# Gated edges of a graph network: one product of 96 rows, four gather buffers, and another wait for GpSimd

## What is computed

```
concat = jnp.concatenate([h[src], h[dst], edge_attr], axis=-1)
gates = jax.nn.sigmoid(concat @ W_e + b_e)
messages = jax.nn.softplus(concat @ W_n + b_n)
gated = gates * messages
h_new = jax.ops.segment_sum(gated, dst, num_segments=n)
edge_count = jnp.clip(edge_count, 1.0, None)[:, None]
return h + h_new / edge_count
```

## Time and profile before

| | us |
|---|---|
| median of 3 runs | 3195.6 (3194.36 to 3196.31) |
| profiled execution, its own time | 3192.49 |
| its span | 3190.5 |
| busy: TensorE, VectorE, ScalarE, GpSimd | 2649.9, 1684.4, 1362.8, 905.0 |
| line 1136, 804 gathers | 766.6 busy |
| line 1349, 1620 records of matmul | 587.0 busy |
| line 1182, 135 adds | 183.8 busy, 402.2 idle before them |

### The profile page before, as it was taken

How to read it: one execution, slowest core, us unless ns; L and a number is a source line. 1 busy time by engine, 2 the same in 40 slices (tenths; PEclk the granted TensorE clock), 3 DMA queues, 4 the chain that set the end, 5 groups by cost and what they waited for, 6 DMA issues and landing times. The chain is left out here.

```text
span 3190.5 us, 66017 instructions
## 1 busy us (share of the span) xinstructions
PE 2649.9 (83%) x21196; PEld 2400.0 (75%) x21197; DVE 1684.4 (53%) x3606; ACT 1362.8 (43%) x2809; POOL 905.0 (28%) x1144
## 2 busy tenths in 40 slices
PE   3888889869999998678777788777877769859999
PEld 2877778759999996666666666666766657649999
DVE  7877787773444436544444444444444452345555
ACT  2544445423333334344444444444444431207776
POOL 2112121200000000566655666566655600000000
PEclk7999999979999998555555555555555569878999
DMA  2333333320000002444434443443334360028272
GB/s 65 118 101 102 102 114 103 101 76 2 2 2 2 2 2 78 119 106 102 103 101 103 106 103 101 101 107 101 104 100 103 100 242 25 1 85 349 92 260 78
DMA packets 221035, 300.31 MB, mean 94 GB/s; under 512 B 101187, under 2 KB 186662, under 8 KB 215430
## 3 DMA queue, kind: packets, MB, share of 16 engines
q1 hardware_dynamic: 181926, 217.20, 21.3%
q0 software_dynamic: 38880, 79.68, 10.3%
HBM read 225.96 MB, written 70.80 MB: 93 GB/s over the span
## 5 line engine op out<-in xcount | busy, mean ns | idle before, releaser
L1136 POOL DMA_INDIRECT layer_R<-source_terms,layer_srcs x804 | 766.6, 954 | 500.7 <-DVE layer_zp L1182 276.0
L1349 PE MATMUL layer_zp<-layer_Wa,layer_at 64*128 64x192 f32 x1620 | 587.0, 536 | 159.3 <-issue 157.2
L1349 PEld LDWEIGHTS layer_zp<-layer_Wa,layer_at 64*128 64x128 f32 x1620 | 494.9, 325 | 192.2 <-issue 185.7
L540 PE MATMUL build_win<-nodes_x,build_S 128*128 128x200 bf16 x5264 | 502.3, 253 | 126.6 <-DVE nodes_x L457 122.0
L540 PEld LDWEIGHTS build_win<-nodes_x,build_S 128*128 128x128 bf16 x5264 | 443.1, 99 | 181.8 <-DVE nodes_x L457 117.2
L935 PEld LDWEIGHTS layer_acc<-layer_U,graph_CT 128*128 128x128 f16 x6250 | 517.8, 98 | 26.3 <-issue 22.4
L935 PE MATMUL layer_acc<-layer_U,graph_CT 128*128 128x192 f16 x6250 | 522.0, 247 | 18.7 <-DVEq L765 18.7
L1182 DVE TENSOR_TENSOR layer_zp<-layer_zp,layer_R 128x1152 f32<-128x1152 f32 x135 | 183.8, 1361 | 402.2 <-remote 402.2
L1299 ACT ACTIVATE layer_y<-layer_zp 128x1152 f32<-128x1152 f32 x135 | 152.7, 1131 | 475.5 <-DVE layer_zp L1182 461.6
L1373 PEld LDWEIGHTS layer_acc<-layer_hot,layer_G 128*98 128x98 f32 x1644 | 287.2, 288 | 42.7 <-issue 40.3
L1373 PE MATMUL layer_acc<-layer_hot,layer_G 128*98 128x32 f32 x1644 | 292.7, 349 | 19.2 <-issue 5.7
(11 more groups left out here) (244 smaller groups left out, 2808.9 us busy)
## 6 DMA issues: line engine op xcount, KB each, us to landing
layer_ring<-W_blocks SPq DMA_DIRECT2D x41, 1600.0 KB, 7.5
W_blocks<-nodes_x SPq DMA_DIRECT2D x400, 100.0 KB, 1.8
layer_at<-in_attr SPq DMA_DIRECT2D x135, 192.0 KB
C_blocks<-build_Cblk SPq DMA_DIRECT2D x25, 800.0 KB, 3.5
layer_C<-C_blocks SPq DMA_DIRECT2D x25, 800.0 KB, 21.9
layer_rows<-target_rows SPq DMA_DIRECT2D x135, 144.0 KB
layer_R<-source_terms,layer_srcs POOLq DMA_INDIRECT x804
layer_Qs<-target_terms SPq DMA_DIRECT2D x135, 36.0 KB
```

The lines of the kernel that those rows point to most:

```text
L540: mm = pe.matmul(out, S[:, b, part, 2 * i + u, :, :].rearrange("p a z -> p (a z)"), M[:, i, u, :, :].rearrange("p a z -> p (a z)"), start= ...
L1136: nc.gpsimd.indirect_dma_start(R[:, h, u, :], None, P_d, bass.IndirectOffsetOnAxis(ap=at_u, axis=0)).then_inc(s_R[h], 16)
L1349: mm = pe.matmul(out[u], at[:, h, u * P:(u + 1) * P], Wa[:, :], start=(u % 2 == 0), stop=False, skip_group_check=True)
```

## The change

Four things are changed together.

- `propagate` stores Q as it is, in 32 bits (`Q_d`). The casts, the subtractions and the two late rounds of the loop go.
- `gated_edges` stacks attributes (partitions 0 to 63) and a one-hot of 32 rows in 32 bits (partitions 64 to 95) in one tile, `left`, and weights and Q rows in `right`. One 32-bit product of 96 rows takes the place of the two. It waits for one-hot and Q rows as well as for the attributes.
- `R` has four buffers (`LONG` is 4).
- GpSimd waits, from step 4 on, for the add of step s - 4 and, ahead of each even step from 2 on, for the product of step s - 2 (`s_z`).

```diff
@@ propagate, SyncE
-                sp.wait_ge(s_cast, 3 * q + 3)
-                sp.dma_start(Q3_d.rearrange("(k p) f -> p k f", p=P)[:, t, :],
-                             Q3[q % 2].rearrange("p k a f -> p k (a f)")).then_inc(s_qst[q % 2], 16)
+                sp.wait_ge(s_Q, 5 * q + 5)
+                sp.dma_start(Q_d.rearrange("(k p) f -> p k f", p=P)[:, t, :], Qf[q % 2]).then_inc(s_qst[q % 2], 16)
@@ propagate, ScalarE
-                    for q in range(5):
-                        for a in range(3):
-                            if k == 5 * q + SPLIT + a:
...
-                                nc.scalar.activation(Q3[q % 2][:, :, a, :], Qf[q % 2], ACT.Copy).then_inc(s_cast, 1)
@@ gated_edges, SyncE
-                sp.dma_start(rows[:, h, :], row_d[:, bass.ds(s * (SE * P), SE * P)].to_broadcast([QR, SE * P])).then_inc(s_rows[h], 16)
-                sp.wait_ge(s_att, s + 1)
-                sp.sem_inc(s_taken, 1)
-                sp.dma_start(at[:, h, :], attr[:, bass.ds(s * (SE * P), SE * P)]).then_inc(s_at[h], 16)
+                sp.dma_start(rows[DE:DK, h, :], row_d[:, bass.ds(s * (SE * P), SE * P)].to_broadcast([QW, SE * P])).then_inc(s_rows[h], 16)
                 sp.wait_ge(s_z, s + 1)
                 sp.sem_inc(s_taken, 1)
-                sp.dma_start(Qs[:, h, :], Qrows[bass.ds(b * 3, QR), :]).then_inc(s_Qs[h], 16)
+                sp.dma_start(left[0:DE, h, :], attr[:, bass.ds(s * (SE * P), SE * P)]).then_inc(s_at[h], 16)
+                sp.dma_start(right[DE:DK, h, :], Q_d[bass.ds(b, QW), :]).then_inc(s_Qs[h], 16)
@@ gated_edges, GpSimd
             for s in range(NS):
-                h = s % 2
+                i = s % LONG
                 if s == 1:
                     pool.wait_ge(s_srcs, 16)
-                pool.wait_ge(s_add, s + 1)
+                if s >= LONG:
+                    pool.wait_ge(s_add, s + 3 - LONG)
+                if s >= 2 and s % 2 == 0:
+                    pool.wait_ge(s_z, s + 1)
...
-                        R[:, h, u, :], None, P_d,
-                        bass.IndirectOffsetOnAxis(ap=at_u, axis=0)).then_inc(s_R[h], 16)
+                        R[:, i, u, :], None, P_d,
+                        bass.IndirectOffsetOnAxis(ap=at_u, axis=0)).then_inc(s_R[i], 16)
@@ gated_edges, VectorE
-                nc.vector.tensor_scalar(hotT[:, h, :, :].rearrange("p u e -> p (u e)"), rows[:, h, :],
-                                        offs[0:QR, bass.ds(s, 1)], None, ALU.is_equal).then_inc(s_hT, 1)
+                nc.vector.tensor_scalar(left[DE:DK, h, :], rows[DE:DK, h, :], offs[DE:DK, bass.ds(s, 1)], None,
+                                        ALU.is_equal).then_inc(s_hT, 1)
...
-            for words in (zp[1][:, :, 0:D2], gate, z[:, :, :, :], y[:, :, :, :], G[:, :, :, 0:D + 1], hot[:, :, :, :]):
+            for words in (zp[1][:, :, 0:D2], gate, z[:, :, :, :], y[:, :, :, :], G[:, :, :, 0:D + 1], hot[:, :, :, :],
+                          leftx[:, :], rightx[0:DE, :]):
@@ gated_edges, TensorE
                 pe.wait_ge(s_ms, s + 2)
                 pe.wait_ge(s_at[h], pair * 16 + 16)
-                for u in range(SE):
-                    mm = pe.matmul(out[u], at[:, h, u * P:(u + 1) * P], Wa[:, :], start=(u % 2 == 0), stop=False,
-                                   skip_group_check=True)
-                mm.then_inc(s_att, 1)
+                pe.wait_ge(s_hT, s + 3)
+                pe.wait_ge(s_Qs[h], pair * 16 + 16)
+                for u in range(SE - 1):
+                    pe.matmul(out[u], left[:, h, u * P:(u + 1) * P], right[:, h, :], start=(u % 2 == 0), stop=False,
+                              skip_group_check=True)
...
-                pe.wait_ge(s_hT, s + 3)
-                pe.wait_ge(s_Qs[h], pair * 16 + 16)
-                for u in range(SE):
-                    mm = pe.matmul(out[u], hotT[:, h, u, :], Qs[:, h, :], start=False, stop=True, skip_group_check=True)
-                mm.then_inc(s_z, 1)
+                u = SE - 1
+                pe.matmul(out[u], left[:, h, u * P:(u + 1) * P], right[:, h, :], start=False, stop=True,
+                          skip_group_check=True).then_inc(s_z, 1)
```

More of the change, by code:

```diff
@@ L635, in layernorm_relu, with propagate @@
     do(nc.vector.scalar_tensor_tensor(out, out, 0.0, rstd.unsqueeze(2).to_broadcast([P, NT, D]), ALU.max, ALU.mult))
-def propagate(nc, x_in, x, CT, indeg, src_cols, We, be, Wn, bn, ident, first, P_d, Q3_d):
+def propagate(nc, x_in, x, CT, indeg, src_cols, We, be, Wn, bn, ident, first, P_d, Q_d):
     D2 = 2 * D
@@ L643, in propagate @@
     TURN, PROD = 7, 8
-    SPLIT = 4 + PROD
-    STEPS = NT + SPLIT - 2
+    STEPS = NT + PROD
     with ExitStack() as ctx:
@@ L813, in last_step @@
                         normal(4)
-                    for q in range(5):
-                        for a in range(2):
-                            if k == 5 * q + SPLIT + 1 + a:
-                                target_rest(q, a)
                     t = k - PROD
@@ L886, in last_step @@
                         deviation(4)
-                    for q in range(5):
-                        for a in range(3):
-                            if k == 5 * q + SPLIT + a:
-                                if a == 0:
-                                    act.wait_ge(s_Q, 5 * q + 5)
-                                    if q >= 2:
-                                        act.wait_ge(s_qst[q % 2], q // 2 * 16)
-                                else:
-                                    act.wait_ge(s_rest, 2 * q + a)
-                                nc.scalar.activation(Q3[q % 2][:, :, a, :], Qf[q % 2], ACT.Copy).then_inc(s_cast, 1)
             def step(nxt, n):
@@ L995, in gated_edges @@
         strides = m.sb("strides", [P, NP // QW + 1], F32)
-        thirdI = m.sb("thirdI", [P, 1], I32)
-        third = m.sb("third", [P, 1], F32)
-        Wa = m.sb("Wa", [DE, D2], F32)
+        place = m.sb("place", [P, 1], F32)
         count = m.sb("count", [P, NT], F32)
-        at = m.sb("at", [DE, 2, SE * P], F32)
-        rows = m.sb("rows", [QR, 2, SE * P], I16)
-        Qs = m.sb("Qs", [QR, 2, D2], BF16)
-        Qx = m.sb("Qx", [QR, D2], BF16)
-        R = m.sb("R", [P, 2, SE, D2], F32)
+        left = m.sb("left", [DK, 2, SE * P], F32)
+        right = m.sb("right", [DK, 2, D2], F32)
+        leftx = m.sb("leftx", [DK, SE * P], F32)
+        rightx = m.sb("rightx", [DK, D2], F32)
+        rows = m.sb("rows", [DK, 2, SE * P], I16)
+        R = m.sb("R", [P, LONG, SE, D2], F32)
         hot = m.sb("hot", [P, 2, SE, QW], F32)
@@ L1027, in gated_edges @@
         s_Qs = [m.sem(f"target_terms_loaded{h}") for h in range(2)]
-        s_R = [m.sem(f"source_terms_gathered{h}") for h in range(2)]
+        s_R = [m.sem(f"source_terms_gathered{i}") for i in range(LONG)]
         s_taken = m.sem("waits_taken")
@@ L1086, in _ @@
             sp.dma_start(dstI[:, :], dst_cols[:, 0:TS]).then_inc(s_dst, 16)
-            sp.dma_start(Wa[:, 0:D], We[2 * D:, :]).then_inc(s_wa, 16)
-            sp.dma_start(Wa[:, D:], Wn[2 * D:, :]).then_inc(s_wa, 16)
+            for h in range(2):
+                sp.dma_start(right[0:DE, h, 0:D], We[2 * D:, :]).then_inc(s_wa, 16)
+                sp.dma_start(right[0:DE, h, D:], Wn[2 * D:, :]).then_inc(s_wa, 16)
             sp.dma_start(ew[:, :], w_cols[:, 0:TS]).then_inc(s_wa, 16)
@@ L1177, in onehots, with add @@
                                         ALU.is_equal).then_inc(s_hot, 1)
-            def add(h, s, pair):
-                dve.wait_ge(s_R[h], (pair * 16 + 16) * SE)
+            def add(h, i, s, turn):
+                dve.wait_ge(s_R[i], (turn * 16 + 16) * SE)
                 dve.wait_ge(s_z, s + 3)
-                nc.vector.tensor_tensor(zp[h][:, :, 0:D2], zp[h][:, :, 0:D2], R[:, h, :, :], ALU.add).then_inc(s_add, 1)
+                nc.vector.tensor_tensor(zp[h][:, :, 0:D2], zp[h][:, :, 0:D2], R[:, i, :, :], ALU.add).then_inc(s_add, 1)
             def logs(h, s):
@@ L1231, in step @@
                 logs(1 - h, s - 1)
-                add(h, s, pair)
+                add(h, i, s, turn)
                 if not last:
@@ L1246, in _ @@
             dve.wait_ge(s_c, 3)
-            do(nc.vector.tensor_scalar(thirdI[:, :], thirdI[:, :], 7, None, ALU.logical_shift_right))
-            do(nc.vector.tensor_copy(third[:, :], thirdI[:, :]))
             dve.wait_ge(s_dst, 32)
-            do(nc.vector.tensor_scalar(offs[:, :], base[:, :], third[:, :], None, ALU.add))
+            do(nc.vector.tensor_scalar(offs[:, :], base[:, :], place[:, :], None, ALU.add))
             do(nc.vector.tensor_copy(dstF[:, :], dstI[:, :]))
@@ L1333, in _ @@
             pe.wait_ge(s_init, 1)
-            pe.wait_ge(s_wa, 48)
+            pe.wait_ge(s_wa, 80)
             pe.wait_ge(s_tab, 16)
```

40 lines of the change are left out of this document (14 added, 26 removed).

## The result

The changed kernel takes 3204.7 us (median of 22 runs, 3196.3 to 3236.0), the kernel before 3194.5 beside it (22 runs, 3189.6 to 3197.4). The ratio is 1.0042, 95% interval 1.0028 to 1.0055: slower by 0.4%, about 13 us, where 3099 was forecast. The runs now lie 40 us apart, before they lay within 8. The profiled execution is the slowest of them (3236.0), so its rows show the loss at its largest.

A forecast was written before the change was run, and what follows sets the result against it. A loop of waits, 18.84 us a pair with TensorE's late count, was taken to bound the kernel. -90 - 8 + 2 = -96 on 3192.5 gave 3096, with 3.1 for the median 3099 us; range 2935 to 3270, likeliest case 3050 to 3145.

The forecast's parts named there:

- What bounds the kernel: Gated-edges stage: a loop of count, add, GpSimd's release, twelve gathers and a late TensorE count, 18.84 us a pair.
- TensorE slow in itself (3300): Rival: TensorE takes 0.69 us a record, gathers or not; 20.5 us a pair, 3300 us; no chance of its own.
- its backlog (2935): Rival: the delay is TensorE's own backlog, so less work ends it; 15.05 us a pair, 2935 us; to 3000: 0.17.
- GpSimd's wait, -90 us: Even steps' gathers wait for the product, not the add behind it: 1.37 us off each of 66 intervals, -90 us.
- One product, cost nothing on the path: Gated-edges products: one of 12 records, 4.20 us, replaces two; 154 us off TensorE's busy time, none on the loop.
- One-hot: VectorE's 32-bit one-hot: 0 to 0.2 us longer, covered; slowing of gathers beside it at most 46 us, taken as 0.
- Loads: SyncE's three loads a step: the two remaining wait for the product alone and land in time, free.
- End of propagation and start: Propagation's end without three-way splitting, -8 us; start and end of the gated-edges stage, +2 us.
- the one on the slower side: Rival: aggregate held until 17.2 us puts accumulate, G and logs before the even add, +90 us; slower altogether 0.38.
- The rival of the late odd count: Rival: the odd product's count is seen late in the twelve gathers; 3202 to 3270 at 0.18, 3500 if fully held.
- Signs: Right: GpSimd pauses 2.6 us, odd adds 6.3 after even, pairs 17.5; wrong: VectorE idle before odd adds or accumulate, clock not 0.5.

The follow-up runs named there:

- few_gathers_before: The kernel before with one gather a step in place of six, the add reading that one column six times: ratio 0.9079.
- wait_alone: The kernel before with only the four buffers and GpSimd's new wait, the two products kept: ratio 1.0131.
- two_products_wait_every: The kernel before with four buffers and GpSimd waiting ahead of every step, odd ones too, for the product of two steps before: ratio 0.9827.
- product_alone: The changed kernel with the old wait, on the add of two steps before, ahead of every step's gathers: ratio 0.9986.
- delayed_start: The changed kernel with five iotas between the new wait and the first gather of an even step: ratio 0.9976.
- half_delay: The changed kernel with three iotas between the new wait and the first gather of an even step: ratio 0.9865.
- paced_200: The changed kernel without the even wait, one iota of 128x200 behind each gather, gathers 1.44 us apart: ratio 0.9783.
- no_even_wait: The changed kernel without GpSimd's wait for the even product: ratio 1.0023.

## Why the prediction was wrong

- *What bounds the kernel* held: the loop, its 18.84 us, and that TensorE's counts and not its work are late (few_gathers_before). That the late count comes with the gathers was assumed, and is now shown. TensorE slow in itself (3300) and its backlog (2935) both fall.
- *GpSimd's wait, -90 us*, is the step that failed. The add that was "taken out of the loop" also held the rows back till VectorE had reached it, whatever had made VectorE late. Waiting for the product alone, a row starts as soon as the count is there while the add is up to 4 us off. Then odd product and aggregate end deeper in the row and are held. wait_alone puts the part at +1.3% (about 42 us), not -2.8%. The early start alone is not enough for the loss: two_products_wait_every starts its rows as early (0.72 us behind the even add's start) and gains. What failed is the silent premise that odd product and aggregate stay prompt when the rows move against them. A smaller miss stands beside it: GpSimd's release was taken at 0.26 us, its time after the add's end, also where it now waits for TensorE's count; there it is 0.72 (two_products_wait_every) and 0.74 (the changed kernel). With 0.72, 14.91 and 2.35 the forecast's own pattern is 17.98 us and not 17.47, so 34 of the 90 us were never there.
- *One product, cost nothing on the path*: nearly right. Its 12 records take 4.20 us as priced (1920.76 to 1924.96), and product_alone's odd add comes 6.30 us after the even one (1906.48, 1912.78), as forecast. What I called covered was covered: a count 4.6 us in is not held.
- *One-hot*: 0.65 us on average, not 0.6 at most, and the contention is there in part. In product_alone, the first gather of a row, beside the one-hot, takes 1.19 us in place of 0.99; its gathers have a mean of 626.02/641 = 0.977 us, before 0.952. That is 0.3 us a pair or 20 us, between the 0 taken and the bound of 46. By the Trainium skill (SBUF — State Buffer, "Who interferes with whom") GpSimd and a VectorE in a two-port mode share a port that the first to issue keeps for its whole instruction, and the other is blocked. The traces agree for a one-hot that is first: where 0.37 us of it lie beside the gather (product_alone) the gather is 0.24 longer than its usual 0.95, where 0.48 do (delayed_start, 1.31) it is 0.36 longer, all but 0.12 of the overlap each time. In the other order they are mixed: in two_products_wait_every a one-hot that starts 0.56 us into a gather (1888.93) takes 0.57 us in place of 0.41, one that starts 0.39 us in (1895.21) takes 0.41. The cost stays small because so little of them overlaps. In the changed kernel the gathers' mean is 954 ns, as before. Against these 0.3 us product_alone's even count comes 0.44 sooner (1.96 against 2.40), which no term of the sum had.
- *Loads* free: right. *End of propagation and start*, -6: the stage's second pair starts 6.6 us earlier.
- *Rivals*: the one on the slower side named the place (the aggregate held behind the gathers, accumulate, G and logs between count and even add) and gave it +90 us. The wait is there, 315 us at line 1175, and the stretch from count to even add is longer than the 2.7 priced (4.84). But the long waits, of nearly 10 us, stand in every second pair, and the pairs in which they stand are the short ones; the loss comes in the pair behind. In all it is 44 us in the slowest run, 10 in the median of the runs. The rival of the late odd count came too: in the long pair the odd add starts 15.1 us behind the first gather (1929.45). It had 3202 to 3270 at a chance of 0.18, and 3205 lies just inside that only because long and short pairs mix. I gave the slower side 0.38. The forecast was put ahead of it on the argument that TensorE would have gaps where it had a long row of work. few_gathers_before shows a full TensorE with prompt counts, and the changed kernel the reverse, an aggregate held to 1913.64 while TensorE stands idle (8.54 us ahead of 1915.57), so that argument was empty. Rows 9 had the two late counts in plain sight, and they belonged in front.
- *Signs*: pauses of 2.6 us were forecast, 3.4 and 7.4 are seen in the pairs shown; odd adds come 6.3 us after the even in the short pairs, as forecast, and 11.0 in the long one (1918.48, 1929.45); the sign for the failure, idle ahead of the accumulate, is the one that came. The granted clock was 0.52, from 0.50.

## What to carry to other kernels

A wait that is redundant on paper may be what keeps two engines in step. Before a producer is released earlier, ask where in its next stretch each count of the others will now fall, and price the case that the pattern does not hold. A loop of waits can have more than one steady pattern: look at a row of its periods one by one, for a mean of 19.7 us hid pairs of 18.1 and 22. Where a count comes late beside a long row of indirect gathers, try spacing the gathers a little: here 0.19 us more for each bought 2.4% of the program without the even wait, and 1.1% of the kernel before.

## What the runs showed of the hardware

- Counts that TensorE sends while GpSimd issues gathers back to back (1.25 us apart) can stay unseen till 2.0 to 2.7 us after the last gather; over 30 gathers an aggregate was used 22.5 us after TensorE began it. Others are held 3 to 5 us and seen in the middle of the row (half_delay). With one gather a step they are seen at once.
- The spacing matters: in the changed kernel without its even wait, 1.28 us apart the even count is held in every pair, at 1.44 and more no wait for a count is left. In the kernel before, some are still held at 1.44. What in the chip holds them no view here shows, nor why a count 7 us into a row passes in one pattern and one of 5 to 7 us does not in another.
- More GpSimd work made the kernel faster: 810 iotas, 263.6 us busy, and 2.4% less time (paced_200 against no_even_wait).
- GpSimd starts 0.26 us after VectorE's add ends when it waits for the add (before), and 0.72 to 0.74 us after VectorE is seen to go on when it waits for TensorE's count (two_products_wait_every, the changed kernel).
